# Spectral slots taken in pairs: the channel mix on half arrays, with 512 columns moving and two result banks added at read-out

## The reference, cut to what matters

```python
Vf   = rfft(phi, n=8192)                       # phi: (L, K), K = 16 filters
Uf_p = rfft(u, n=8192);  Uf_m = rfft(u * sgn)  # u: (2, L, 128)
U_plus, U_minus = irfft(Vf * Uf_p), irfft(Vf * Uf_m)
out  = einsum('btkd,k,kde->bte', U_plus,  s, Mpp)
out += einsum('btkd,k,kde->bte', U_minus, s, Mpm)
```

## Time and profile before

| | us |
|---|---|
| median of 3 runs | 3382.94 |
| lowest, highest | 3381.09, 3384.28 |
| the profiled execution, its own time | 3384.74 |
| its span from first to last instruction | 3383.0 |
| first matmul of the stage | at 1213.2 |
| last matmul of the stage starts | at 2402.45 |
| mean granted TensorE clock, whole span | 0.95 |

### The profile page before, as it was taken

The page is one execution under the profiler, slowest core; times in us unless marked ns, Lnnn a source line. Parts: engine busy times, 40 slices in busy tenths (PEclk is TensorE's granted clock), DMA queues, the critical chain, the costliest instruction groups (busy, mean ns, idle before and its releaser), DMA issues. The chain is left out here.

```text
span 3383.0 us, 60840 instructions
## 1 busy us (share of the span) xinstructions
PE 3071.9 (91%) x23047; PEld 2397.8 (71%) x23047; DVE 1908.1 (56%) x3737; ACT 1419.0 (42%) x3058; POOL 1056.3 (31%) x1104
## 2 busy tenths in 40 slices
PE   5999997688873989999999999999889998999699
PEld 4777775233432568888888888888868887888555
DVE  5556585577525345555555555555336776776365
ACT  2555553111232234444444444444125666667200
POOL 3445450377521044444444444444000000000000
PEclk9999998799986999999999999999779999999799
DMA  7988850000002355454545455554200000000000
GB/s 173 186 181 181 179 152 20 13 1 1 1 3 109 140 74 76 72 79 69 79 72 82 72 76 76 73 79 69 62 6 1 1 1 1 1 1 1 8 22 28
DMA packets 407112, 213.33 MB, mean 63 GB/s; under 512 B 313972, under 2 KB 386316, under 8 KB 405036
## 3 DMA queue, kind: packets, MB, share of 16 engines
q1 hardware_dynamic: 388960, 199.27, 30.9%
q10 hardware_dynamic: 17868, 10.19, 1.4%
HBM read 177.82 MB, written 52.89 MB: 68 GB/s over the span
## 5 line engine op out<-in xcount | busy, mean ns | idle before, releaser
L1670 DVE TENSOR_TENSOR sl_vl_slot<-sl_psV_slot,sl_vh_slot 128x512 fp32r<-128x512 f32 x1024 | 636.1, 684 | 563.8 <-ACT sl_vh_slot L1649 563.8
L1649 ACT ACTIVATE sl_vh_slot<-sl_psV_slot 128x512 fp32r<-128x512 f32 x1024 | 529.3, 604 | 584.4 <-PE sl_psV_slot L1617 584.4
L85 PE MATMUL sl_psY_slot<-sl_vl_slot,sp_Mh_sp 128*128 128x256 f32 x2048 | 603.9, 295 | 0.0
L86 PE MATMUL sl_psY_slot<-sl_vh_slot,sp_Ml_sp 128*128 128x256 f32 x2048 | 577.8, 282 | 0.0
L87 PE MATMUL sl_psY_slot<-sl_vh_slot,sp_Mh_sp 128*128 128x256 f32 x2048 | 576.8, 282 | 0.0
L85 PEld LDWEIGHTS sl_psY_slot<-sl_vl_slot,sp_Mh_sp 128*128 128x128 f32 x2048 | 389.1, 190 | 91.0 <-issue 90.6
L86 PEld LDWEIGHTS sl_psY_slot<-sl_vh_slot,sp_Ml_sp 128*128 128x128 f32 x2048 | 390.4, 191 | 0.0
L87 PEld LDWEIGHTS sl_psY_slot<-sl_vh_slot,sp_Mh_sp 128*128 128x128 f32 x2048 | 389.8, 190 | 0.0
L1593 POOL CAST sl_fh_slot<-sl_f_slot 128x512 fp32r<-128x512 f32 x256 | 167.3, 653 | 575.5 <-PE sl_psV_slot L1617 575.5
L1595 POOL TENSOR_TENSOR sl_fl_slot<-sl_f_slot,sl_fh_slot 128x512 fp32r<-128x512 f32 x256 | 337.8, 1319 | 20.6
L2025 DVE TENSOR_TENSOR ca_ptl_ca<-ca_psT_ca,ca_pth_ca 128x512 fp32r<-128x512 f32 (+1 forms) x272 | 183.8, 676 | 170.3 <-ACT ca_pth_ca L1962 170.2
(11 more groups left out here) (395 smaller groups left out, 6180.6 us busy)
## 6 DMA issues: line engine op xcount, KB each, us to landing
sl_f_slot<-filt_hat SPq DMA_DIRECT2D x256, 256.0 KB, 5.4
na_v_na<-na_windows SPq DMA_DIRECT2D x128, 390.0 KB
na_windows<-na_values SPq DMA_DIRECT2D x160, 113.8 KB, 6.4
na_values<-na_vo_na ACTq DMA_DIRECT2D x32, 260.0 KB, 6.7
u_hat<-fw_o_fwd SPq DMA_DIRECT2D x8, 1024.0 KB, 3.8
sl_u_slot<-u_hat SPq DMA_DIRECT2D x128, 64.0 KB, 2.2
y_hat<-sl_y_slot SPq DMA_DIRECT2D x128, 64.0 KB, 4.7
X<-in_x SPq DMA_DIRECT2D x8, 512.0 KB, 8.1
```

The costliest lines, as they stand in the source:

```text
L85: e.matmul(out, lh, rl, start=start, stop=False)
L86: e.matmul(out, ll, rh, start=False, stop=False)
L1649: e.activation(v_out(0, n, q), bank(4 * n + q), ACT.Copy).then_inc(S["v_high"], 1)
L1670: e.tensor_tensor(v_out(1, n, q), bank(m), v_out(0, n, q), ALU.subtract).then_inc(S["v_split"], 1)
```

## The change

Slots are taken in pairs. Chunk n now belongs to slot `n // 8 * 2 + n % 2`, so that neighbouring chunks hold the same filters' positions of the two slots of a pair, and both lie side by side in one `v` buffer.

The mix works on groups of two chunks. The 128 channels are contracted in two halves of 64 rows, one into `psY[0]`, the other into `psY[1]`, and each matmul moves 512 columns: 256 of each slot. A group has 48 such matmuls in two parts of 24. The two banks are added at read-out: ACT copies `psY[0]` out, DVE adds `psY[1]`. Both banks serve every pair of slots, so `psY` has a single buffer. Filters are loaded chunk by chunk (four DMAs of 64 KB each) into a ring of four. The split filters have two buffers instead of three. PE has three convolutions ahead of the first mix.

```diff
-    CHUNKS = SLOTS * KC
-    NPV, NFI, NVR, EARLY = 6, 3, 3, 8
+    PAIRS, GROUPS, CHUNKS = SLOTS // 2, SLOTS // 2 * KC, SLOTS * KC
+    NPV, NFI, NFR, EARLY = 6, 2, 4, 8
+    HALF, KM = R // 2, KN // 2
+    slot_of = lambda n: (n // (2 * KC) * 2 + n % 2, n // 2 % KC)
...
-        f_raw = [sb(f"sl_f{i}", [128, NF, 2, R]) for i in range(2)]
+        f_raw = [sb(f"sl_f{i}", [128, KN, 2, R]) for i in range(NFR)]
-        v = [[sb(f"sl_v{p}{i}", [128, KN, CH], F32R) for p in "hl"] for i in range(NVR)]
-        y_sb = [sb(f"sl_y{i}", [128, B * 128]) for i in range(2)]
+        v = [[sb(f"sl_v{p}{i}", [128, 2, KN, CH], F32R) for p in "hl"] for i in range(2)]
+        y_sb = [sb(f"sl_y{i}", [128, 2 * B * 128]) for i in range(2)]
-        psY = [pb(f"sl_psY{i}", [128, B * 128]) for i in range(2)]
+        psY = [pb(f"sl_psY{i}", [128, CH]) for i in range(2)]
...
+                def load_f(n):
+                    if n >= NFR:
+                        e.wait_ge(S["f_split"], n - NFR + 1)
+                    u, kc = slot_of(n)
                     for i in range(2):
...
+                for n in range(CHUNKS):
+                    p, at = divmod(n, 2 * KC)
+                    if n + NFR < CHUNKS:
+                        load_f(n + NFR)
+                    if at < 2 and p + 1 < PAIRS:
+                        load_u(2 * p + 2 + at)
+                    if at == 4 and p >= 1:
+                        store(p - 1)
...
-                def mix(n):
-                    u, kc = divmod(n, KC)
-                    e.wait_ge(S["v_split"], 4 * (n + 1))
-                    if kc == 0 and u >= 2:
-                        e.wait_ge(S["y_out"], u - 1)
-                    for k in range(KN):
+                def mix(g, part):
+                    p, kc = divmod(g, KC)
+                    if part == 0:
+                        e.wait_ge(S["v_split"], 8 * (g + 1))
+                        if kc == 0 and p >= 1:
+                            e.wait_ge(S["y_out"], 2 * p)
+                    for k in range(part * KM, (part + 1) * KM):
                         for x in range(2):
-                            right = [t[:, k, :].rearrange("p (q x c) -> p q x c", q=2, x=2)[:, :, x, :] for t in v[n % NVR]]
+                            right = [t[:, :, k, :].rearrange("p i (q x c) -> p q i x c", q=2, x=2)[:, :, :, x, :] for t in v[g % 2]]
                             left = [G[m][x][:, kc * KN + k, :] for m in ("Mh", "Ml")]
-                            mm = product(e, psY[u % 2][:, :], left, right, kc == 0 and k == 0 and x == 0,
-                                         kc == KC - 1 and k == KN - 1 and x == 1)
+                            for z, (pl, pr) in enumerate(((0, 1), (1, 0), (0, 0))):
+                                for half in range(2):
+                                    rows = slice(half * R, (half + 1) * R)
+                                    mm = e.matmul(psY[half][:, :], left[pl][rows, :], right[pr][rows],
+                                                  start=kc == 0 and k == 0 and x == 0 and z == 0,
+                                                  stop=kc == KC - 1 and k == KN - 1 and x == 1 and z == 2)
...
-                convolve(0)
-                convolve(1)
+                for n in range(3):
+                    convolve(n)
+                for g in range(GROUPS):
+                    for part in range(2):
+                        mix(g, part)
+                        if 2 * g + part + 3 < CHUNKS:
+                            convolve(2 * g + part + 3)
...
+                def outputs(p):
+                    e.wait_ge(S["mixed_s"], 2 * KC * (p + 1))
+                    if p >= 2:
+                        e.wait_ge(S["y_stored"][p % 2], 64 * (p // 2))
+                    for q in range(2):
+                        e.activation(y_part(p, q), y_bank(0, q), ACT.Copy).then_inc(S["y_half"], 1)
...
             def _(e):
+                def outputs(p):
+                    for q in range(2):
+                        e.wait_ge(S["y_half"], 2 * p + q + 1)
+                        y = y_part(p, q)
+                        e.tensor_tensor(y, y_bank(1, q), y, ALU.add).then_inc(S["y_out"], 1)
```

More of the change, by code:

```diff
@@ L1510, in spectral_slots @@
         u_raw = [sb(f"sl_u{i}", [128, B, 128]) for i in range(2)]
-        f_raw = [sb(f"sl_f{i}", [128, NF, 2, R]) for i in range(2)]
-        u_in = [[sb(f"sl_u{p}{i}", [128, B, 128], F32R) for p in "hl"] for i in range(2)]
+        f_raw = [sb(f"sl_f{i}", [128, KN, 2, R]) for i in range(NFR)]
+        u_in = [[sb(f"sl_u{p}{i}", [128, B, 128], F32R) for p in "hl"] for i in range(4)]
         f_in = [[sb(f"sl_f{p}{i}", [128, CH], F32R) for p in "hl"] for i in range(NFI)]
-        v = [[sb(f"sl_v{p}{i}", [128, KN, CH], F32R) for p in "hl"] for i in range(NVR)]
-        y_sb = [sb(f"sl_y{i}", [128, B * 128]) for i in range(2)]
+        v = [[sb(f"sl_v{p}{i}", [128, 2, KN, CH], F32R) for p in "hl"] for i in range(2)]
+        y_sb = [sb(f"sl_y{i}", [128, 2 * B * 128]) for i in range(2)]
         psV = [pb(f"sl_psV{i}", [128, CH]) for i in range(NPV)]
-        psY = [pb(f"sl_psY{i}", [128, B * 128]) for i in range(2)]
-        S = Stage(nc, ctx, [("slot_loaded", 2), "u_high", "u_split", "f_high", "f_split", "v_in_psum_s", "v_high", "v_split",
-                            "mixed_s", "y_out", ("y_stored", 2), "y_early"])
+        psY = [pb(f"sl_psY{i}", [128, CH]) for i in range(2)]
+        S = Stage(nc, ctx, [("u_loaded", 2), ("f_loaded", NFR), "u_high", "u_split", "f_high", "f_split", "v_in_psum_s",
+                            "v_high", "v_split", "mixed_s", "y_half", "y_out", ("y_stored", 2), "y_early"])
         def v_out(part, n, q):
             b, par = divmod(q, 2)
-            return bass.AP(v[n % NVR][part], 128 * par + 64 * b, [[KN * CH, 128], [CH, KN], [384 - 256 * par, 2], [1, 64]])
+            return bass.AP(v[n // 2 % 2][part], n % 2 * KN * CH + 128 * par + 64 * b,
+                           [[2 * KN * CH, 128], [CH, KN], [384 - 256 * par, 2], [1, 64]])
+        y_bank = lambda half, q: psY[half][:, q * 256:(q + 1) * 256].rearrange("p (m r) -> p m r", r=HALF)
+        y_part = lambda p, q: y_sb[p % 2][:, :].rearrange("p (m r q) -> p q m r", r=HALF, q=2)[:, q, :, :]
         bank = lambda m: psV[m % NPV][:, :].rearrange("p (k q c) -> p k q c", k=KN, q=2)
@@ L1531, in _, with load_u @@
             def _(e):
-                def load(u):
+                def load_u(u):
                     if u >= 2:
                         e.wait_ge(S["u_split"], u - 1)
-                        e.wait_ge(S["f_split"], KC * (u - 1))
                     uh = T["u_hat"][2 * u:2 * u + 2, :, :].rearrange("i (s q) c -> q i s c", q=2)
@@ L1542, in load @@
                         for par in range(2):
[L1543 removed]
+                            src = bass.AP(row.tensor, row.offset + par, [[2, HALF], [2 * R, KN * 2], [1, R]])
                             at = par * R + i * HALF
[L1545 to L1546 removed]
@@ L1548, in store @@
[L1548 to L1553, removed]
+                            e.dma_start(f_raw[n % NFR][at:at + HALF, :, :, :].rearrange("p k o r -> p (k o) r"), src)\
+                                .then_inc(S["f_loaded"][n % NFR], 16)
@@ new lines, in store @@
+                def store(p):
+                    e.wait_ge(S["y_out"], 2 * (p + 1))
+                    for i in range(2):
+                        u = 2 * p + i
+                        for b in range(B):
+                            at = (i * B + b) * 128
+                            e.dma_start(T["y_hat"][2 * u:2 * u + 2, b, :, :].rearrange("o e r -> e o r"),
+                                        y_sb[p % 2][:, at:at + 128].rearrange("e (o r) -> e o r", o=2))\
+                                .then_inc(S["y_stored"][p % 2], 16)
@@ L1555, in load_early @@
                 def load_early(group):
                     for i in range(2):
-                        e.wait_ge(S["y_stored"][i], 32 * (EARLY // 2) * (group + 1))
+                        e.wait_ge(S["y_stored"][i], 64 * (EARLY // 4) * (group + 1))
                     rows = slice(2 * EARLY * group, 2 * EARLY * (group + 1))
                     e.dma_start(G["y0"][rows, :], T["y_hat"][rows, 0, :, :].rearrange("c e r -> c (e r)")).then_inc(S["y_early"], 16)
-                load(0)
-                load(1)
@@ L1563, in _ @@
[L1563 to L1570, removed]
+                for u in range(2):
+                    load_u(u)
+                for n in range(NFR):
+                    load_f(n)
+                for n in range(CHUNKS):
[6 more added lines that the diff above has]
+                        store(p - 1)
+                    if at == 6 and p % (EARLY // 2) == 1 and p > EARLY // 2:
+                        load_early(p // (EARLY // 2) - 1)
@@ L1577, in split_input @@
                 def split_input(u):
[L1578 to L1581, removed]
+                    e.wait_ge(S["u_loaded"][u % 2], 32 * (u // 2 + 1))
+                    if u >= 4:
```

(19 more changed lines are left out.)

21 lines of the change are left out of this document (7 added, 14 removed).

## The result

The changed kernel takes 3246.97 us (median of 4 runs, 3241.03 to 3252.85) against 3382.02: a ratio of 0.9601, 95% interval 0.958 to 0.9621, 135 us less. The forecast was 109 less, 3274, with a range of 3258 to 3305. Two later rounds beside the kernel before gave 0.9598 and 0.9594.

The account below looks back on a forecast made before the run. TensorE alone was taken to bound the kernel. Turns and streaming -117 us, result banks +8, head -2 and tail +2 sum to -109, taking the median from 3382.9 to about 3274; range 3258 to 3305.

Parts of the forecast that it names:

- What bounds the kernel: In the changed stage, TensorE alone sets the pace: busy 200.00 us of 200, at 4.64 us a chunk.
- The turns: On TensorE, where convolution and mix follow one another: changing array shape costs 0.385 us a chunk, all of it saved.
- The rival that the gap was a wait or a bank: Gaps between mix and convolution stay; only 18 us saved, less 8, giving 3373 us; chance 0.06.
- Streaming: In the mix on TensorE: 12 pairs of halves at 0.2325 us, 2.79 against 2.86, saving 0.07 us a chunk.
- a faster pair: Rival: steps of a pair of halves shrink below 0.2325, for instance to 0.22, 57 us more saved, 3217; chance 0.03.
- Result banks: First mix of a slot pair waits for the previous pair's read-out of `psY`: 0.25 us, 31 times, 8 us added.
- Evacuation: DVE's copying out of a convolution's chunk before its mix: 1.4 us of cover, cost 0.
- POOL: Splitting filters on POOL with two buffers instead of three: 3.7 us of cover, cost 0.
- SP: Issuing 32 filter DMAs instead of 8 per pair of slots: 23.6 us of its 33.4, cost 0.
- the rival on SP: At 0.89 us per filter DMA, issuing takes 34.7 against 33.4 us a pair, giving 3316 us; chance 0.05.
- The DMA share: Sign on the DMA engines in the stage: bytes stay the same, busy share goes from 0.48 to 0.53.
- Head and tail: Stage start and end: earlier first matmul, later first mix, net -2 us; one more copy, sums and stores, +2 us.

## Why the prediction was right, and where it was wrong

*What bounds the kernel.* Right: TensorE alone, before and after, at a granted clock of 1.00.

*The turns, 0.385 us a chunk.* Right in place, cause and nearly in size. The turns are gone; the full-array mix brings them back, at 0.40; two kernels that differ in the rows of one small matmul differ by 0.35. The rival that the gap was a wait or a bank, 0.06, is excluded.

*Streaming: "I take 0.2325".* This is the step that failed. In the changed kernel a pair of halves takes 0.2267, in mix and convolution alike. The 0.2325 was right for the row that it was read from, pairs two to six of a run of six, and wrong for a stream of 144 steps from one boundary to the next. The term is 18 x (0.2325 - 0.2267) = 0.104 us a chunk, 27 us in 256, and this is the miss: 109 + 27 = 136, against 135 measured, and 136 and 138 in the later rounds. I had kept this as the rival "a faster pair", with 0.03, for which the price was about right in kind (0.22 and 3217) and the chance was not. Its condition, no turns between, was not the right one either: the step is 0.232 without a turn in the half arrays with 256 columns, and 0.227 with one in the run with the small matmul on 128 rows. What the runs show is that 0.2267 is the settled step; what sets the longer ones ahead of it stays open.

The rows that would have told were there. In the causal attention of the kernel before, nine full-array matmuls of 512 columns stand in a row behind some of 256, with no change of shape:

```profile
2578.39 0.28 PE L87 MATMUL ca_psO_ca<-ca_pth_ca,ca_vh_ca 128*128 128x256 f32 x1
2578.51 0.40 PE L85 MATMUL ca_psS_ca<-ca_kl_ca,ca_qh_ca 128*128 128x512 f32 x1
...
2579.67 0.39 PE L87 MATMUL ca_psS_ca<-ca_kh_ca,ca_qh_ca 128*128 128x512 f32 x1
...
2580.35 0.40 PE L87 MATMUL ca_psS_ca<-ca_kh_ca,ca_qh_ca 128*128 128x512 f32 x1
```

The first five steps, 2578.51 to 2579.67, are 0.232, and the next three, to 2580.35, are 0.227. And the full-array steps of the earlier trace rows are 0.1191 on the mean of 22, but the last 14 of them, from 1803.97 to 1805.65, are 0.120:

```profile
1803.97 0.28 PE L85 MATMUL sl_psY_slot<-sl_vl_slot,sp_Mh_sp 128*128 128x256 f32 x1
```

At 2.4 GHz 256 columns take 0.1067, so a settled step costs 0.0133 beside its columns. Put on 512 columns, 0.2133, that is 0.2266. The same sum on 0.2325 gives 0.019, and two figures for one overhead should have made me ask which of them was settled. Measured now: 0.120 at 256 columns and 0.2267 at 512, with one matmul or two in a step, both 0.0133 above the columns.

The Trainium skill ("TensorE: Matmul & The Clock Gate", Back-to-back issue gap) gives, for the isolated gap, the columns at 2.4 GHz and some 2.5 ns. By the page's figure a step of 512 would be an estimated 0.216. The runs here, all in fp32r, show 13.3 ns and no step of 0.216; the measurement decides.

*Result banks, +8.* Right in mechanism, 2 us too small: the stall is 0.28 us for my 0.25, and the ten longer steps behind it, which I had not counted, make it 0.33, 10 us in 31. Two kernels without the wait are 10.5 and 9.0 us faster, the first although its first mix starts 2.6 us later. My times for the read-out held to some hundredths (ACT at T + 0.44 for 0.42, DVE's end at T + 1.64 for 1.60 to 1.68).

*Evacuation, POOL, SP: nothing.* Right. A filter DMA of 64 KB takes 0.451 us to issue (median) and lands after 2.2. The 0.89 of the rival on SP was one slot's; the median of the 256 KB DMAs before is 0.587. No row has TensorE wait for POOL or DVE in the running stage, but for the sum of the read-out. The DMA share, however, did not rise to 0.53: it fell from 0.48 to 0.41, at 84 GB/s for 72.

*Head and tail.* From the first DMA issue to the first mix it was 18.0 us and is 16.1, with one convolution more done: 3.3 better than before, forecast -2 for the net. From the start of the last matmul to the next stage's first DMA it was 3.8 us and is 5.8: 2 more, as forecast.

*The range.* Its lower end holds a slip: without a stall at the banks the saving of my own sum is 117 and not 121, and so 3266 and not 3262. The time lies below either.

In sum: turns and streaming together 0.56 us a chunk, 143 less; boundary 10 more; head 3 less; tail 2 more; 134 less in all, which is what the stage lost in the two traces (first DMA to the next stage's: 1206.1 and 1072.4 us).

## What to carry to other kernels

A step read from a run of six matmuls holds for a run of six. When a change makes the run longer, take the step from the end of the longest run of that size in the trace, wherever in the program it stands, or split it into the columns at the granted clock and a fixed part and check the fixed part against another size. And where a contraction of 64 rows alternates with one of 128, the alternation has a price of its own (0.2 us a turn here), which half arrays for both remove without a loss in the stream, at the price of a second result bank and its read-out (10 us here); a single small matmul of the other shape brings it back.

## What was not expected of the hardware

- The first steps of 512 columns are longer (0.232 instead of 0.227) in several places, and then they settle: five in the full-array mix from 1801.37, five in the convolution behind a mix of 256 columns without any gap (from 1800.63), five in the causal attention before (from 2578.51), ten behind the wait at a boundary (from 1805.59). Behind the small full-array matmul there are none, though a change of shape lies there. What sets them stays open; nothing was run to tell.
- Two halves with a weight load each step by 0.120 us at 256 columns, as one full-array matmul with one load does.
